# Last cross-attention of a Perceiver block: the first 512 keys are turned by TensorE instead of loaded turned, the mask is spread by ScalarE, and a round is cut in two parts

## The reference, cut to what matters

```python
x = x + _L3_xattn_ref(_layernorm(x), ctx, ctx, Wq, bq, Wk, bk, Wv, bv, mask)

q = query @ Wq + bq;  k = ctx @ Wk + bk;  v = ctx @ Wv + bv
scores = einsum('bsd,btd->bst', q, k) / sqrt(128)
scores = where(mask, -1e9, scores)              # mask is [32, 64, 1601]
y = einsum('bst,btd->bsd', softmax(scores, axis=2), v)
```

## Time and profile before

| | us |
|---|---|
| time, median of 3 runs (2854.63 to 2857.21) | 2854.74 |
| the profiled execution | 2865.53 |
| its span | 2863.70 |
| L3_xattn in that span | 2412.67 to 2589.49 |

### The profile page before, as it was taken

How to read it: one execution, slowest core, us unless ns; L and a number is a source line. 1 busy time by engine, 2 the same in 40 slices (tenths; PEclk the granted TensorE clock), 3 DMA queues, 4 the chain that set the end, 5 groups by cost and what they waited for, 6 DMA issues and landing times. The chain is left out here.

```text
span 2863.7 us, 74292 instructions
## 1 busy us (share of the span) xinstructions
PE 2513.6 (88%) x30990; PEld 1696.0 (59%) x31020; DVE 1929.0 (67%) x6295; ACT 1409.0 (49%) x2625; POOL 433.6 (15%) x304
## 2 busy tenths in 40 slices
PE   7998854898999999999999999999879998988543
PEld 5776743555777466666666666666545555665323
DVE  5554423675211588888888888889578885666776
ACT  3442313664333355555555555555479952434521
POOL 1000022540000100000000000000008920644200
PEclk9998977998999899999999999999689999999866
DMA  7980131000000100000100000100012202990000
GB/s 228 330 295 11 53 120 37 9 3 18 15 23 8 55 26 26 26 26 27 36 25 26 25 26 26 33 29 3 9 41 96 96 23 97 350 347 9 2 0 15
DMA packets 73374, 189.52 MB, mean 66 GB/s; under 512 B 12130, under 2 KB 39717, under 8 KB 73008
## 3 DMA queue, kind: packets, MB, share of 16 engines
q1 hardware_dynamic: 64912, 156.68, 16.8%
q10 hardware_dynamic: 7104, 26.23, 2.6%
q0 software_dynamic: 1024, 1.85, 0.2%
HBM read 154.19 MB, written 30.79 MB: 65 GB/s over the span
## 5 line engine op out<-in xcount | busy, mean ns | idle before, releaser
L3284 DVE CUSTOM_DVE_ANT_0 L_xattn_junk<-L_xattn_ps_mx,L_xattn_shift 128x512 f32<-128x512 f32 (+1 forms) x1024 | 544.7, 569 | 140.4 <-issue 139.9
L3355 ACT ACTIVATE L_xattn_pT<-L_xattn_ps_st 128x512 f32<-128x512 f32 x768 | 417.0, 595 | 352.7 <-PE L_xattn_ps_st L3112 231.2
L3127 PE MATMUL L_xattn_ps_mx<-L_xattn_kT,L_xattn_qb 32*128 32x512 f32 (+1 forms) x2048 | 514.2, 554 | 1.2 <-DVE L_xattn_tops L3284 1.2
L3112 PE MATMUL L_xattn_ps_st<-L_xattn_qb,L_xattn_kT 32*128 32x256 f32 (+1 forms) x3328 | 471.8, 383 | 0.0
L3322 DVE TENSOR_TENSOR L_xattn_pT<-L_xattn_pT,L_xattn_capT 128x1024 f32<-128x1024 f32 (+1 forms) x325 | 362.1, 1115 | 18.3 <-ACT L_xattn_pT L3355 15.9
L3112 PEld LDWEIGHTS L_xattn_ps_st<-L_xattn_qb,L_xattn_kT 32*128 32x128 f32 (+1 forms) x3328 | 341.2, 185 | 7.0
L3177 PE MATMUL L_xattn_ps_pv<-L_xattn_pT,L_xattn_v 128*17 128x128 f32 x6656 | 266.9, 280 | 0.0
L3177 PEld LDWEIGHTS L_xattn_ps_pv<-L_xattn_pT,L_xattn_v 128*17 128x17 f32 x6656 | 150.8, 98 | 144.4 <-issue 114.4
L3127 PEld LDWEIGHTS L_xattn_ps_mx<-L_xattn_kT,L_xattn_qb 32*128 32x128 f32 x2048 | 169.3, 185 | 32.0 <-DVE L_xattn_tops L3284 27.2
L3139 PE MATMUL L_xattn_ps_st<-L_xattn_less,L_xattn_ones_b 3*128 3x512 bf16 x768 | 187.7, 390 | 0.4 <-ACT L_xattn_pT L3355 0.4
L3050 POOL TENSOR_TENSOR L_xattn_qb<-ln_sq,L_xattn_four 128x256 f32<-128x256 f32 x32 | 20.5, 643 | 994.7 <-PE L_xattn_ps_st L3112 989.3
(11 more groups left out here) (633 smaller groups left out, 4906.5 us busy)
## 6 DMA issues: line engine op xcount, KB each, us to landing
L_xattn_ctxT<-context_turned SPq DMA_DIRECT2D x64, 800.5 KB, 6.5
context_turned<-L_xattn_ctxT SPq DMA_DIRECT2D x32, 800.5 KB, 9.6
L_xattn_ctx<-in_ctx SPq DMA_DIRECT2D x32, 768.0 KB
L_xattn_ctx<-in_ctx ACTq DMA_DIRECT2D x32, 768.0 KB
L_attn_cc<-scratch_rows SPq DMA_DIRECT2D x32, 512.0 KB, 3.6
L_xattn_out_keys<-scratch_q SPq DMA_DIRECT2D x32, 200.1 KB, 10.1
L_ffn_w<-in_L_ffn_w SPq DMA_DIRECT2D x4, 1024.0 KB, 10.8
L_ffn_w<-in_L_ffn_W SPq DMA_DIRECT2D x16, 256.0 KB, 3.0
```

The lines of the kernel that those rows point to most:

```text
L3112: last = nc.tensor.matmul(st[0:chunk[j], w % 3, 256 * c2:256 * c2 + 256], kT[n % 3][r:r + 32, P * j:P * j + chunk[j]], qb[n % 3][r:r + 32, ...
L3127: last = nc.tensor.matmul(mx[:, w % 3, to:to + width], qb[n % 3][32 * g:32 * g + 32, 2 * (p % 2):2 * (p % 2) + 2, :].rearrange("p h q -> p ...
L3284: last = nc.vector.tensor_tensor_reduce(out=junk[:, w % 3, to:to + width], in0=mx[:, w % 3, to:to + width], in1=shift[:, k0:k0 + width], s ...
L3355: nc.scalar.activation(pT[b % HELD][:, :, gi, :], st[:, w % 3, :].rearrange("p (c k) -> p c k", c=2), ACT.Exp)\
```

## The change

The three straight buffers become four. The turned buffer is split: keys 0 to 511 are no longer loaded turned, TensorE turns them from the straight context (8 transposes a round, `turn_context`), ScalarE copies the first batch's and VectorE the second batch's half out of PSUM; the other 1089 keys are loaded turned as before (`rest`, 1.12 MB a round). All loads are now issued by SyncE, the straight ones too; the straight load of round r+1 waits for M of tile r-3. GpSimd does nothing any more: the mask is spread by two ScalarE activations of the same shapes (`spread_mask`). They wait for mask and turned rest together, which share a semaphore. The order of a pass changes: result of r-3, p of r-2, projection of r-3, M of r-2, S of r, so that p of a tile comes two passes behind its scores. There is one more pass at the end.

```diff
-        ctx = s.sb("ctx", [P, 3, 2, KC, D])
-        ctxT = s.sb("ctxT", [P, 3, 2, KEYS])
+        ctx = s.sb("ctx", [P, 4, 2, KC, D])
+        ctxT, rest = s.sb("ctxT", [P, 2, 2, 512]), s.sb("rest", [P, 3, 2, KEYS - 512])
...
             for r in range(NT):                                  # SyncE
                 if r >= 3:
                     sp.wait_ge(out_made, r - 2)
+                    sp.wait_ge(*PE.at(f"S3_{r - 3}"))
                 load_mask(r)
+                if r < 3:
+                    load_context(r)
+                load_turned(r)
                 if r == 1:
                     sp.dma_start(ahead.w[:, :], a[f"{ahead_name}_w"]).then_inc(ahead.loaded, 16)
-                if r >= 3:
-                    sp.wait_ge(*PE.at(f"S3_{r - 3}"))
-                load_turned(r)
+                if r >= 2 and r + 1 < NT:
+                    if r >= 3:
+                        sp.wait_ge(*PE.at(f"M3_{r - 3}"))
+                    load_context(r + 1)
-        @block.gpsimd
...
+            def turn_context(r, b):                              # TensorE
+                unit = f"T{b}0_{r}"
+                if b == 0:
+                    pe.wait_ge(ctx_in[r % 4], 64 * (r // 4) + 64)
+                if turn_of[unit] >= 3:
+                    pe.wait_ge(*emptied(unit))
+                for j in range(4):
+                    last = nc.tensor.transpose(bank(unit)[:, P * j:P * j + P], ctx[:, r % 4, b, j, :], c.ident[:, :])
+                last.then_inc(PE.did(unit), 1)
...
+            for r in range(NT + 3):
+                scoring, mixing, finishing = r < NT, 2 <= r < NT + 2, r >= 3
+                if scoring:
+                    turn_context(r, 0)
+                    turn_context(r, 1)
...
+                if finishing:
+                    turn_result(r - 3)
+                if mixing:
+                    for g in range(NG):
+                        turn_probs(r - 2, g)
+                if finishing:
+                    project(r - 3)
+                if mixing:
+                    for g in range(NG):
+                        mix(r - 2, g)
+                if scoring:
+                    for g in range(NG):
+                        score(r, g)
...
-            for r in range(3):                                   # ScalarE
-                load_context(r)
             ln_scalar(c, act, V, A, PE, tp)
+            def spread_mask(r):
+                act.wait_ge(kept_in[r % 3], 64 * (r // 3) + 64)
+                if r >= 3:
+                    act.wait_ge(*V.at(f"s3_{r - 3}"))
+                nc.scalar.activation(in_turn_of_chunks(out_[:, r % 3, :]), in_turn_of_keys(mask[:, r % 3, :]), ACT.Copy, scale=OUT)
+                nc.scalar.activation(out_[:, r % 3, REST:KEYS], mask[:, r % 3, REST:KEYS], ACT.Copy, scale=OUT).then_inc(out_made, 1)
```

More of the change, by code:

```diff
@@ L3599, in kept_cross_attention @@
     wide = [w for _, w in SPANS]
+    turns = [u for r in range(NT + 2) for u in [f"T00_{r}", f"T10_{r}"] * (r < NT) + [f"qk{g}" for g in range(NG)] * (r == 0) +
+             [f"p{g}_{r - 2}" for g in range(NG)] * (r >= 2)]
+    turn_of = {u: n for n, u in enumerate(turns)}
     with Stage(c, name) as s:
@@ L3627, in kept_cross_attention @@
[L3627 to L3631, removed]
@@ L3646, in load_turned, with load_context @@
                 for b in (0, 1):
-                    sp.dma_start(ctxT[:, r % 3, b, :], c.turned[2 * r + b, :, :]).then_inc(turned_in[r % 3], 16)
+                    sp.dma_start(rest[:, r % 3, b, :], c.turned[2 * r + b, :, 512:KEYS]).then_inc(kept_in[r % 3], 16)
+            def load_context(r):
+                for b in (0, 1):
+                    keys = a["ctx"][2 * r + b, :, :]
+                    sp.dma_start(ctx[:, r % 4, b, 0:KC - 1, :], keys[0:REST, :].rearrange("(p j) d -> p j d", p=P)).then_inc(ctx_in[r % 4], 16)
+                    sp.dma_start(ctx[0:KREST, r % 4, b, KC - 1, :], keys[REST:KEYS, :]).then_inc(ctx_in[r % 4], 16)
             def load_mask(r):
                 for b in (0, 1):
-                    sp.dma_start(mask[S * b:S * b + S, r % 3, :], a[mask_name][2 * r + b, :, :]).then_inc(mask_in[r % 3], 16)
+                    sp.dma_start(mask[S * b:S * b + S, r % 3, :], a[mask_name][2 * r + b, :, :]).then_inc(kept_in[r % 3], 16)
             for r in range(NT):
@@ L3682, in _ @@
                     .then_inc(PE.did(f"q{i}"), 1)
[L3683 to L3692, removed]
+            def turn_context(r, b):
[7 more added lines that the diff above has]
+                last.then_inc(PE.did(unit), 1)
             def mix(r, g):
[L3695 to L3698, removed]
+                if g == 0 and r > 0:
+                    pe.wait_ge(*V.at(f"o_{r - 1}"))
                 pe.wait_ge(*(V if g == 3 else A).at(f"p{g}_{r}"))
@@ L3739, in project @@
                 nc.tensor.matmul(small[:, P:2 * P], oT[:, :], wv[:, :], start=True, stop=True).then_inc(PE.did(f"out_{r}"), 1)
[L3741 to L3746, removed]
+            for r in range(NT + 3):
[3 more added lines that the diff above has]
+                    turn_context(r, 1)
+                if r == 0:
+                    for i in range(4):
+                        pe.wait_ge(*V.at(f"q{i}"))
+                        if turn_of[f"qk{i}"] >= 3:
+                            pe.wait_ge(*emptied(f"qk{i}"))
+                        nc.tensor.matmul(bank(f"qk{i}"), wkT[:, :], qT[:, 512 * i:512 * i + 512], start=True, stop=True)\
+                            .then_inc(PE.did(f"qk{i}"), 1)
+                    for t in range(NT):
+                        last = nc.tensor.matmul(small[:, t:t + 1], qT[:, P * t:P * t + P], bk[:, :], start=True, stop=True)
+                    last.then_inc(PE.did("qbk"), 1)
+                    pe.wait_ge(*A.at("qk3"))
                 if finishing:
-                    turn_result(r - 2)
-                for g in range(NG) if using else ():
-                    turn_probs(r - 1, g)
+                    turn_result(r - 3)
+                if mixing:
+                    for g in range(NG):
+                        turn_probs(r - 2, g)
                 if finishing:
-                    project(r - 2)
+                    project(r - 3)
[5 more added lines that the diff above has]
+                        score(r, g)
         @block.vector
```

151 lines of the change are left out of this document (80 added, 71 removed).

## The result

| | before | changed |
|---|---|---|
| median of 12 runs each, us | 2855.74 | 2869.74 |
| lowest and highest, us | 2850.83, 2869.08 | 2860.51, 2885.18 |
| ratio with 95% interval | | 1.0041 [1.0024, 1.0057] |
| L3_xattn in the profiled execution, us | 177.1 | 190.3 |
| round, third M to fourteenth, us | 9.64 | 10.39 |

Predicted were 2849.8 us and a range of 2845 to 2863. The two profiled executions are of nearly one span (2863.7 and 2864.8 us), but in the second the stages ahead, whose code is the same, took 12.5 us less; that is difference between executions. So this text compares the stage by its own length: the first instruction of TensorE in it to the first of the next stage, 2412.72 to 2589.82 before, 2400.21 to 2590.50 after. It is 13.2 us longer, 0.46% of the time, which agrees with the ratio.

The account below looks back on a forecast made before the run. Loads bound the changed stage at 361 GB/s; afterwards TensorE (8.85 us a round) and the loop (8.8) would, taken as 8.95. The stage ends 4.9 us earlier: 2854.74 - 4.9 = 2849.8 us, range 2845 to 2863.

Parts of the forecast that it names:

- this very loop: SyncE's in-order loads, the spread, T00's copy, p1 and M wait on each other over two passes: 17.55 us, 8.8 a round.
- one rate for copy and exp, whatever it reads: ScalarE's spread of the mask takes 1.75 us, priced at its rate for copy and exp.
- Abs and Sign: On ScalarE, once behind the spread of pass 4, they delay T00's copy by 2.2 us and p1 by 1.9.
- Clock dips like the one above should go: TensorE would not idle, so drops of its clock behind waits should vanish; already contained in the 9.64 us round.
- the spread is slow: ScalarE's spread takes 3.3 us at half rate (2857.6 us in all) or 5.5 at GpSimd's rate (2872); chance 0.17.
- one queue is slower: SyncE's single queue carries 324 GB/s: transfer 9.1 us, loop 9.25 a round, 2853.7 us in all; chance 0.2.
- p1 and p2 stall: TensorE's p1 and p2 wait for copies by ScalarE and VectorE: a pass of 9.5 us, 2857 in all; chance 0.11.
- TensorE: Eight more transposes a round cost 0.95 us on top of 7.90: a round of 8.85 us.
- VectorE: Some 5.5 of 8.85 us busy, on no path; its 70-column step, 4.71 us beside GpSimd's spread, falls under 1.
- Start: Without load issues on ScalarE the norm gains 5.2 us, T of round 0 adds 0.95; scores begin at 2435.4.
- First passes: Pass 1 ends about 2444.3; in pass 2 p1 waits 0.9 us, and the pass ends at 2453.5.
- End: Behind the last score the same work stands as before, 12.8 us; the stage ends at 2584.6.

Follow-up runs that it names:

- the kernel with both edits: The changed kernel with mask and turned rest issued before the straight load and the mask on its own semaphore: ratio 0.9977 to the kernel before, round 8.79 us.
- the kernels with the loop open: Six variants of the changed kernel: mask and rest issued earlier, mask on its own semaphore, spread on GpSimd, or combinations, one with two queues: ratios 0.9962 to 0.9980.
- the early order with GpSimd: The changed kernel with mask and turned rest issued before the straight load and the spread given back to GpSimd: ratio 0.9975 to the kernel before, round 8.57 us.
- two queues: The changed kernel with mask and rest issued earlier and straight loads of tiles 3 to 15 issued by GpSimd: ratio 0.9980 to the kernel before, round 8.54 us.
- the early order: The changed kernel with mask and turned rest issued before the wait for M and the straight load: ratio 0.9979 to the kernel before, round 8.48 us.

## Why the prediction was wrong, step by step

*The failed step is SyncE's.* The prediction wrote down this very loop, and summed it to 17.55 us, 8.8 a round. Measured it is 20.74 in the mean of eleven turns (20.8 in the one shown). Two of its terms were mis-sized. The batch, "start of a DMA 2.0" and "transfer 8.2", 10.2 together, is 12.4: 1.1 a round. One full queue carries 331 to 344 GB/s in the kernel with both edits and not 361 (some 8.7 us in place of 8.2), and in the loop it is not full. At 2514 to 2517, between two batches, the changed kernel shows a DMA share of 0.53:

```profile
2514.00:2517.00 3.00, 3.00 (x26) 1.28 (x22) 1.78 (x7) 0.49 (x1) 0.00 (x0) 1.00 0.53 174
```

The last pieces of one batch land until 2516.51 while the next, issued at 2514.53, has not begun to move at full rate. The first batch of the loop was issued, at 2442.14, when the DMA engines stood idle (share 0.01 in the microsecond before), and took 11.25 us; the later ones took 11.4 to 13.9. How this divides between starts, ends and the batch ahead was not separated. The other term is the spread: 2.3 us from its start to T00's copy and not 1.75, as "one rate for copy and exp, whatever it reads" is refuted: 0.3 a round. Abs and Sign, which the prediction counted apart, and T00's copy waiting for TensorE in two of the turns add another 0.3. The issue, 0.2 for 0.3, and the copy to the end of M, 5.2 for 5.3, give 0.1 back; in the turn shown, at full clock, the latter is 4.9. Together 1.6 a round, from 8.8 to 10.4.

*The clock was put at nothing.* "Clock dips like the one above should go", said the prediction, since TensorE would not idle. With the loop closed it idled, the granted clock was 0.97 over eleven rounds, and the matmuls took 4.7 us longer. With the loop open it was 1.00 from 2460 to 2540 in five of the six kernels (0.98 in the early order with GpSimd), as the prediction said.

*The rival "the spread is slow" had the right place and too small a price.* By its own point of decision (2.1 us of spread) 2.3 to 2.5 us cost 0.1 to 0.2 a round, 1.3 to 2.6 in 13. What it left out is that the forecast had 0.05 us of room between loop and TensorE's round: any error in any term of the loop went into the round. This rival and that of the slower queue were each priced alone, with all other terms at the forecast's, and never together. Behind it stood the rule of the Trainium skill, "Advanced Engine Details and Errata", section Memory Cachelines, that an access moving to another 16-byte line each time is penalised. The rows agree: 2.30 against 1.485 us, no half rate but 0.65 of the full one.

*The rival "one queue is slower" was half right.* 324 GB/s was its figure; a full queue shows 336 to 342 over 80 us of this stage. Alone it is worth 0.0 to 0.3 a round, as the kernels with the loop open show (8.48 to 8.79). The rule cited from the Trainium skill, "Trainium Kernel Development and Optimization", section Key Constraints, that several issuing engines save only issue time, would have given 361 by one queue too. The rows do not bear that out, but they don't refute the rule either: with the same loads two queues show 350, which is 2 to 4% more than one, and the rest of the gap is there with two queues as well.

*The rival "p1 and p2 stall" did not happen.* Where p1 waited it was for the spread ahead of the copy. With the loop open, and p1 and p2 behind the same copies as before, passes are 8.48 us.

*TensorE.* A free pass is 8.48 us and not 8.85: the prediction's error here was on the good side. The eight transposes take 0.93 us, predicted 0.95; the rest of the pass takes 7.55 in place of 7.90, and why was not looked into. *VectorE* as predicted: the 70-column step takes 0.187 us, not 4.71. It wins nothing as long as the loop holds. *Start.* First scores at 22.63 us of the stage, 26.89 before, 4.26 nearer; predicted 4.25. But the reason was half a reason: taking the issues from ScalarE doesn't do it while GpSimd's spread falls on the norm. *First passes.* p1 of pass 2 waited 2.61 us and not 0.9, and M behind it took 4.68 at a lowered clock. *Abs and Sign* held p1 of pass 5 up for 2.64 us, of them some 2.2 their own; predicted 1.9. *End.* 12.5 us from the last score to the stage's last instruction, predicted 12.8.

The sum: the stage is 18.1 us longer than predicted (190.3 for 172.2). Passes 0 to 2 are 3.7 of them (44.5 for 40.8), passes 3 to 15 are 14.6 (132.9 for 118.3, Abs and Sign in both), and the end gives 0.3 back.

## What to carry to other kernels

A loop of waits that comes within a few per cent of the bound is the forecast's largest risk: price each of its terms from the slow side, and ask of each load in it whether it has to be behind that wait. Here neither the order (mask and rest behind the straight load) nor the shared semaphore was needed, and leaving out either one turns 0.4% slower into 0.2 to 0.4% faster. A semaphore that counts two loads makes its waiter wait for both; an instruction moved to an in-order engine makes all behind it wait for its loads, however short it is itself.

## What the runs showed of the hardware

- ScalarE reads 1-byte elements 12 bytes apart in 2.30 us for 1536 columns, contiguous in 1.485 (0.967 ns a column; the step from copy to exp is 0.955).
- GpSimd's spread of 4.8 us held two kinds of VectorE instruction up for nearly its whole length: the norm's (4.96 us for 0.60) and the quantising step (4.71 for 0.187), both tensor_scalar from SBUF to SBUF. It did not hold up all: beside a spread from 2448.58 to 2453.68, in the early order with GpSimd, a reciprocal took 0.15 us and a tensor_scalar out of PSUM 0.35, as elsewhere.
- At a DMA share of 1.02 to 1.03 the engines moved, over 80 us, 336 to 342 GB/s by one queue and 350 by two with the same loads, and 361 by two with the mix of the kernel before.
- TensorE's granted clock was below full behind waits of 2.6 us (0.72 from 2468 to 2474, 0.63 from 2437.4 to 2442), and M took 3.84 and 4.68 us for 3.06. Not behind every such wait: behind the 2.65 us that end at 2510.07 M took 3.06. In the eleven rounds without waits of the early order it was 1.00.
